# Keys multiplied once with a running maximum, and a ninth count table, in a graph, attention and expert layer on one core

## The chip, the cores and the metric

One core of a Trainium2 chip runs the whole layer in one launch. The metric is the device time of an execution in microseconds (us), the median of several; lower is better. The engines are PE (matrix products), DVE (vector), ACT (scalar functions), POOL (GpSimd) and SP, which here only issues transfers. Each has an instruction stream of its own, and streams wait for each other by semaphores.

## The reference, cut to what matters

```python
xn = layernorm(x)                                     # 6250 nodes x 256
# graph convolution: 100000 edges sorted by dst, plus one loop per node
out = segment_sum((xn @ W)[src] * norm[:, None], dst) + bias
gnn = prelu((out - out.mean()) / (out.std() + eps) * w + b)
# linear attention, 4 heads of 32, four memory keys and values ahead of the nodes'
q, k, v = split(rmsnorm(xn) @ w_qkv, 3)
q = softmax(q, over the 32 features) * 32 ** -0.5
k = softmax(k, over memory and all nodes)
context = sum over nodes of k * v                     # 32 x 32 a head
mix = rmsnorm(context applied to q, @ w_out + b_out) + xn
x = x + gnn + mix
x = x + top-2-of-8 experts(layernorm(x))
```

The edges are sorted by destination, and the low node numbers receive far more of them than the high ones.

## The kernel before, in words

The nodes are 49 tiles of 128 rows, the edges 196 groups of four chunks of 128. A first stage (to 125 us) counts degrees, normalises the rows, writes them to `table` in HBM and keeps them turned as `zT`. The second stage, the one that the change edits, sums neighbours' rows into `acc` and runs the attention beside that. A third applies `W` to `acc`, norms and routes; a fourth runs the experts (from about 920 us).

The second stage treats edge groups in two ways.

- **Tables** (groups 0 to 74, the dense ones). They are cut into eight blocks (`DBLK`). A block's destinations span at most 128 nodes, so its edges become a table of counts `adj`, 128 x 49 tiles x 128, which multiplies the rows of all nodes once. For each chunk of edges DVE makes two one-hot matrices in 16 bits (`chunk_onehots`, L1073 and L1074), PE multiplies them (`count`, L839), and DVE adds the narrow result into the table at a column that it reads from a register (`chunk_add`, L1088). When a block is complete, PE multiplies 49 tiles of the table by 49 tiles of `table` (`product`, L851), which SP loads again for each block into a ring `zrow` of six buffers (`z_rows`, L775). ACT copies the sum out (`block_out`, L1002), PE turns it (`turn_block`, L858), DVE adds it to `acc` (`add_block`, L1066). Two tables alternate; ACT wipes the part that was used (L958), and both whole tables at the start.
- **Steps** (the other 121 groups, `GQ`). For each, POOL gathers four times 128 rows of 1 KB by an indirect transfer (L811; the first two groups, `EARLY`, already at the end of the first stage, L466), into a ring of four groups. DVE makes a 128 x 4 x 96 one-hot (L1045), PE multiplies it with the gathered rows in two halves (`aggregate`, L828), DVE adds the 96-wide result to `acc` (`add`, L1058). POOL's gather for step q waits until PE has done step q - 4.

All other work is dealt out to the steps by hand: `share(q, lo, hi, n)` says which of n items fall to step q, `quarter` which to each quarter of it. The order on each engine is this list. `BUILT` says in which steps a block's chunks are counted, `USED` in which its products are made.

The attention, in the steps:

- From `A0` to `A1` (0 to 11) PE multiplies the keys of all tiles (L865) and DVE takes the maximum (L1099, at the first tile L1095). Two set-up steps turn the maximum into a row and multiply the memory's exponents.
- From `C0` to `C1` (14 to 33) PE multiplies keys and values again (L874), DVE subtracts the maximum (L1106), ACT takes the exponent (L974) and copies the values (L970), PE sums the context (L881).
- From `B0` to `B1` (37 to 87) the queries: two products and a transpose on PE (L888, L896, L902), six instructions on DVE, three on ACT.
- From `D0` to `D1` (91 to 118) the attention's norm; SP loads the tiles of x again into a ring of three (`x_tile`, L781, on the same queue as `z_rows`), ACT scales them (L994), DVE adds (L1154).

The last block is turned ahead of step 119, so its table rows, the last x tile and ACT's copy come ahead of the last aggregations on PE. After the loop SP loads the weights of the next stage; the third stage needs them and `acc`.

```python
BUILT = (0, 33, 47, 61, 74, 86, 95, 104, 112)
USED = (33, 47, 61, 74, 86, 95, 104, 112, GQ - 2)
```

## Time and profile before

| | |
|---|---|
| median of three runs | 1326.18 us (1324.99 to 1328.23) |
| the profiled execution's own time | 1320.53 us |
| its span | 1318.8 us |
| PE, DVE, ACT, POOL busy | 92%, 69%, 41%, 60% |
| second stage | from about 126 to 757 us |
| packets' bytes | 190.10 MB, mean 144 GB/s |

How to read it: the span goes from the first to the last instruction, and what lies around it makes up the execution's time. Busy shares count the time in which an engine executes; waiting and register instructions are left out. A float32 multiplication appears as two matmul records, and their durations overlap, so that what a record takes of PE is read from how closely they follow each other. In the chain of work a piece is followed back to what released it. "issue" is time in which an engine waited for nothing that the profile shows.

### The profile page before, as it was taken

The numbers are of one execution on the slowest core, as the hardware profiler recorded it, in microseconds if no ns is written. First come the engines' busy times: TensorE is split into PE (matmuls) and PEld (weight loads), VectorE is DVE, ScalarE is ACT, GpSimd is POOL, SyncE is SP. The second block draws the span as 40 slices with busy tenths as digits, with TensorE's granted clock in tenths as the row PEclk, the third lists the DMA queues.
The fourth block names the chain that finished last, engine by engine and source line by source line (L and its number), as shares of the span: only waits on it lengthen the run. The fifth ranks groups of instructions, "written<-read, shape, count | busy, mean of one in ns | idle before, by whom it ended". The sixth has DMA issues, their size and how long they took to land.

```text
span 1318.8 us, 29769 instructions
## 1 busy us (share of the span) xinstructions
PE 1206.9 (92%) x8357; PEld 1076.2 (82%) x8358; DVE 911.9 (69%) x2764; ACT 543.8 (41%) x1403; POOL 789.1 (60%) x757
## 2 busy tenths in 40 slices
PE   6974989998999999998998798958999999999998
PEld 6964978887889888887786646945999999999997
DVE  8997987887888778778784268888444444444444
ACT  8837102222333333333321102645555555555553
POOL 7105777777777777777777300003577666667665
PEclk9997999999999999999999899965999999999999
DMA  8026333336666667779998701578354444444443
GB/s 256 0 78 199 100 104 105 103 104 198 193 194 205 195 197 210 207 239 276 281 295 271 259 0 33 176 238 249 57 77 65 70 71 71 70 69 70 69 68 43
DMA packets 138889, 190.10 MB, mean 144 GB/s; under 512 B 22262, under 2 KB 116957, under 8 KB 138533
## 3 DMA queue, kind: packets, MB, share of 16 engines
q0 software_dynamic: 43440, 90.29, 29.6%
q1 hardware_dynamic: 95348, 98.64, 23.6%
q8 instruction: 43, 0.70, 0.2%
q14 instruction: 58, 0.47, 0.1%
HBM read 156.37 MB, written 33.44 MB: 144 GB/s over the span
## 4 chain that ended last, share of the span: by engine, by line
PE 54%; POOL 14%; DVE 9%; issue 7%; DMA 4%; DVEq 2%; ACT 1%; SPq 0%; POOLq 0%
PE ps L1991 14%; PE ps L2001 14%; POOL RG L811 14%; PE ps L828 7%; PE ps L851 4%; PE ps L1534 3%; DMA zrow<-table 2%; PE ps L1571 2%; PE ps L1981 2%; DVE R L1088 2%; PE ps L874 1%; PE ps L1589 1%; DMA RG<-table,srci 1%; PE ps L839 1%; DVEq L1080 1%
## 5 line engine op out<-in xcount | busy, mean ns | idle before, releaser
L811 POOL DMA_INDIRECT RG<-table,srci x476 | 468.4, 984 | 146.8 <-issue 142.9
L828 PEld LDWEIGHTS ps<-S_t,RG 128*128 128x128 f32 x1936 | 255.7, 196 | 21.5 <-DMA RG<-table,srci 11.4
L828 PE MATMUL ps<-S_t,RG 128*128 128x96 f32 x1936 | 258.9, 277 | 8.7 <-DMA RG<-table,srci 8.3
L851 PE MATMUL ps<-zrow,R 128*128 128x256 f32 (+1 forms) x784 | 220.8, 387 | 19.3 <-DMA zrow<-table 12.9
L2116 POOL DMA_INDIRECT out<-R,S_t x105 | 166.1, 1582 | 96.9 <-DVE R L2086 50.3
L1991 PE MATMUL ps<-R,RG 128*128 128x128 f32 x1680 | 204.9, 275 | 0.0
L2001 PE MATMUL ps<-R 128*128 x840 | 198.6, 380 | 0.0
L1991 PEld LDWEIGHTS ps<-R,RG 128*128 128x128 f32 x1680 | 195.9, 192 | 0.2 <-issue 0.2
L2028 ACT ACTIVATE R<-ps,RG 128x128 f32<-128x128 f32 x420 | 119.7, 368 | 177.1 <-PE ps L1991 177.1
L1088 DVE TENSOR_TENSOR R<-R,ps 128x245 f32 (+4 forms) x300 | 141.8, 473 | 69.4 <-PE ps L839 42.6
L2082 DVE TENSOR_TENSOR R<-ps,R 128x256 f32<-128x256 f32 x105 | 44.6, 425 | 202.0 <-PE ps L2001 202.0
L851 PEld LDWEIGHTS ps<-zrow,R 128*128 128x128 f32 (+1 forms) x784 | 135.4, 190 | 46.3 <-DMA zrow<-table 25.6
L2001 PEld LDWEIGHTS ps<-R 128*128 128x128 f32 x840 | 151.8, 191 | 16.2
L958 ACT ACTIVATE R<-iwin 128x256 f32<-128x256 f32 (+2 forms) x152 | 71.3, 476 | 183.7 <-PE ps L851 171.9
L2104 POOL DMA_INDIRECT R<-ntable,S_t x105 | 104.0, 991 | 38.7 <-issue 30.2
L2037 ACT ACTIVATE RG<-R 128x1028 f32 x105 | 112.7, 1075 | 4.1 <-DVEq L1918 4.1
L1684 POOL COPY R<-R 128x8 f32<-128x8 f32 (+1 forms) x13 | 6.5, 517 | 143.5 <-DVEq L1854 124.8
L2071 DVE TENSOR_SCALAR R<-ps,gamma,beta 128x128 f32<-128x128 f32 x212 | 76.0, 399 | 0.0
L487 PE MATMUL ps<-R 128*128 128x49 bf16 x784 | 73.8, 270 | 0.0
L487 PEld LDWEIGHTS ps<-R 128*128 128x128 bf16 x784 | 70.8, 145 | 2.8 <-DVE R L562 2.7
L1045 DVE TENSOR_TENSOR S_t<-dstrel,iwin 128x384 f32<-128x384 f32 x121 | 66.8, 552 | 0.8
L1074 DVE TENSOR_SCALAR ohs<-iokey,slo 128x128 bf16<-128x128 f16 x225 | 61.9, 275 | 0.0
(374 smaller groups left out, 1822.7 us busy)
## 6 DMA issues: line engine op xcount, KB each, us to landing
zrow<-table SPq DMA_DIRECT2D x384, 128.0 KB
RG<-table,srci POOLq DMA_INDIRECT x484, 3.3
ntable<-R SPq DMA_DIRECT2D x12, 516.0 KB, 6.6
out<-R SPq DMA_DIRECT2D x12, 512.0 KB, 3.2
table<-R SPq DMA_DIRECT2D x9, 640.0 KB
R<-in_x SPq DMA_DIRECT2D x6, 896.0 KB, 10.0
R<-in_w SPq DMA_DIRECT2D x8, 514.0 KB, 5.7
slot<-in_x SPq DMA_DIRECT2D x32, 128.0 KB
```

The costliest lines, as they stand in the source:

```text
L487: last = nc.tensor.matmul(ps[7][:, 0:T], ohlo[k][:, :, c], ohhi[k][:, :, c], start=False, stop=False)
L811: nc.gpsimd.indirect_dma_start(out=grows[:, s, :], out_offset=None, in_=table, in_offset=bass.IndirectOffsetOnAxis(ap=srci[:, ND + q, c:c ...
L828: last = nc.tensor.matmul(window(q % 2)[:, h, :], grows[:, s, h * P:(h + 1) * P], S_t[:, q % 2, c, :], start=c == 0, stop=c == GC - 1)
L851: nc.tensor.matmul(psD[:, 0:D], adj[b % 2][0:n, j, :], zrow[0:n, i % ZR, :], start=j == 0, stop=j == T - 1).then_inc(z_used, 1)
L1088: nc.vector.tensor_tensor(win, win, psK[m % 2][:, 0:T * wide].rearrange("p (j w) -> p j w", w=wide), ALU.add).then_inc(cnt_ok, 1)
L1991: last = nc.tensor.matmul(psH[s % 2][:, h * P:(h + 1) * P], w1r[:, s, k * HID + h * P:k * HID + (h + 1) * P], ur[:, s % 2, k, :], start=k ...
L2001: last = nc.tensor.matmul(psY[s % 2][:, 0:D], hr[:, s % 2, h, :], w2_sb[:, bass.ds(e, 1), h, :].rearrange("p a f -> p (a f)"), start=h == ...
L2028: last = act.activation(hr[:, s % 2, h, :], psH[s % 2][:, h * P:(h + 1) * P], ACT.Gelu, bias=w1r[:, s, KC * HID + h:KC * HID + h + 1])
L2037: act.activation(w1r[:, s, :], w1_sb[:, bass.ds(e, 1), :].rearrange("p a f -> p (a f)"), ACT.Copy).then_inc(c_ok, 1)
L2071: nc.vector.tensor_scalar(ur[:, s % 2, k, :], psX[s % 2][:, k * P:(k + 1) * P], gamma[:, k:k + 1], beta[:, k:k + 1], ALU.mult, ALU.add)
L2104: nc.gpsimd.indirect_dma_start(out=xr[:, t % 4, :], out_offset=None, in_=ntable, in_offset=bass.IndirectOffsetOnAxis(ap=gat[:, t:t + 1], a ...
L2116: nc.gpsimd.indirect_dma_start(out=a_out, out_offset=bass.IndirectOffsetOnAxis(ap=sct[:, t:t + 1], axis=0), in_=yr[:, t % 4, :], in_offset ...
```

## The change

Nothing outside the second stage is edited, but for one more block mask in the first stage.

- The groups 75 to 78 become a ninth table, nine columns wide; 117 steps and 468 gathers are left. `BUILT` and `USED` are written anew. `EARLY` is 1: one group's gathers are issued ahead of the barrier between the stages.
- Keys are multiplied once, turned (features on partitions) and in 13 rounds of four tiles. A round k begins at quarter 8 + 9k of the steps: PE multiplies 512 keys (quarter 0) and the values of its four tiles (1 to 4); DVE scales the keys by the nodes' norms, reduces the maximum and updates the running one (2); ACT takes the exponent and the factor by which older sums fade (3); PE turns the exponents (4); ACT copies them and the values (5); PE multiplies the context (7); DVE fades and adds (8).
- The norms, needed along the free dimension, are turned, stored to HBM and loaded as rows by SP into the ring of the table rows; SP begins with `z_rows` only after the last round. Exponents and values use the other buffers of the ring and the slots of x.
- The memory's maximum, exponents and products come first, ahead of the two wipes on ACT.
- The last block is turned after the last step.

```diff
-DBLK = ((0, 27), (27, 38), (38, 46), (46, 53), (53, 59), (59, 65), (65, 70), (70, 75))
+DBLK = ((0, 27), (27, 38), (38, 46), (46, 53), (53, 59), (59, 65), (65, 70), (70, 75), (75, 79))
-DWB = (5, 5, 6, 7, 8, 8, 8, 9)
+DWB = (5, 5, 6, 7, 8, 8, 8, 9, 9)
...
-        EARLY = 2
+        EARLY = 1
...
-        A0, A1 = 0, 12
-        C0, C1 = 14, 34
-        B0, B1 = 37, 88
-        D0, D1 = 91, GQ - 2
-        BUILT = (0, 33, 47, 61, 74, 86, 95, 104, 112)
-        USED = (33, 47, 61, 74, 86, 95, 104, 112, GQ - 2)
+        K0, KD = 8, 9
+        C1 = 32
+        B0, B1 = 35, 87
+        D0, D1 = 90, GQ - 2
+        BUILT = (0, 31, 43, 54, 64, 74, 84, 93, 101, 108)
+        USED = (31, 43, 54, 64, 74, 84, 93, 101, 108, GQ - 2)
...
+        def key_turn(q, r):
+            at = 4 * q + r - K0
+            return [(k, at - KD * k) for k in range(NKS) if 0 <= at - KD * k <= KD]
...
# SP
+                sp.wait_ge(cr_ok, 1)
+                sp.dma_start(cflat.rearrange("(t p) -> t p", p=P), ks4[0:T, 0:P]).then_inc(cr_out, 16)
+                sp.wait_ge(cr_out, 16)
+                for k in range(NKS):
+                    if k >= 2:
+                        sp.wait_ge(k_ok, k - 1)
+                    lo, n = KS * k * P, key_nodes(k)
+                    sp.dma_start(cq_row[k % 2][:, 0:n],
+                                 cflat[lo:lo + n].unsqueeze(0).to_broadcast([P, n])).then_inc(cr_in[k % 2], 16)
+                sp.wait_ge(cx_ok, NKS + 1)
                 for q in range(-2, GQ - 2):
                     for b, j in products(q + 2):
                         z_rows(b, j)
...
# PE
+                def keys(k):
+                    if k >= 1:
+                        pe.wait_ge(et_ok, k)
+                    lo, n = KS * k * P, key_nodes(k)
+                    for half in range(KC):
+                        last = nc.tensor.matmul(psKT[:, 0:n], wqkv[:, half, P:2 * P], zT[:, half, lo:lo + n],
+                                                start=half == 0, stop=half == KC - 1)
+                    last.then_inc(k_ps, 1)
+                def turn_exp(k):
+                    pe.wait_ge(ex_ok, k + 1)
+                    pe.wait_ge(k_top, k + 1)
+                    for j, t in enumerate(key_tiles(k)):
...
+                def context(k):
+                    pe.wait_ge(et_ok, k + 1)
+                    pe.wait_ge(v_ok, key_tiles(k)[-1] + 1)
+                    pe.wait_ge(cx_ok, k + 1)
...
                 def attention(q, r):
+                    if q == 0 and r == 0:
+                        nc.tensor.transpose(psT[0:T, :], cq[:, :], ident[:, :])
+                        pe.wait_ge(mem_ok, 1)
+                        nc.tensor.transpose(psKT[0:MEM, 0:P], emk, ident[:, :])
+                        nc.tensor.transpose(psKT[0:MEM, P:2 * P], mvv[:, :], ident[:, :]).then_inc(pre_pe, 1)
+                    if q == 0 and r == 3:
+                        pe.wait_ge(pre_dve, 1)
+                        nc.tensor.matmul(psC[:, 0:P + 1], emT[:, :], mvT[:, :], start=True, stop=True).then_inc(cx_ps, 1)
+                    for k, at in key_turn(q, r):
+                        if at == 0:
+                            if k == 0:
+                                pe.wait_ge(cr_ok, 1)
+                            keys(k)
+                        if 1 <= at <= len(key_tiles(k)):
+                            values(KS * k + at - 1)
+                        if at == 4:
+                            turn_exp(k)
+                        if at == 7:
+                            context(k)
...
                 for q in range(GQ):
-                    if q in USED[1:]:
+                    if q in USED[1:-1]:
                         turn_block(USED.index(q) - 1)
...
+                turn_block(NDB - 1)
# ACT
+                act.wait_ge(m_ok, 1)
+                act.activation(emk, mk[:, :], ACT.Exp, bias=negM[0]).then_inc(mem_ok, 1)
+                act.wait_ge(pre_pe, 1)
+                act.activation(ks4[0:T, 0:P], psT[0:T, :], ACT.Copy).then_inc(cr_ok, 1)
                 for b in range(2):
                     wipe(b, 0, T).then_inc(clear, 1)
...
+                def keys_exp(k):
+                    act.wait_ge(m_ok, k + 2)
+                    n = key_nodes(k)
+                    act.activation(fade[k % 2], negM[k % 2], ACT.Exp, scale=-1.0, bias=negM[(k + 1) % 2])
+                    act.activation(ks4[:, 0:n], ks4[:, 0:n], ACT.Exp, bias=negM[(k + 1) % 2]).then_inc(ex_ok, 1)
...
# DVE
+                def keys_scaled(k):
+                    n = key_nodes(k)
+                    v.wait_ge(k_ps, k + 1)
+                    v.wait_ge(cr_in[k % 2], k // 2 * 16 + 16)
+                    if k >= 1:
+                        v.wait_ge(et_ps, k)
+                    nc.vector.tensor_tensor(ks4[:, 0:n], psKT[:, 0:n], cq_row[k % 2][:, 0:n], ALU.mult).then_inc(k_ok, 1)
+                    v.wait_ge(k_ok, k + 1)
+                    nc.vector.tensor_reduce(ktop, ks4[:, 0:n], AX.X, ALU.max).then_inc(k_top, 1)
+                    v.wait_ge(k_top, k + 1)
+                    nc.vector.scalar_tensor_tensor(negM[(k + 1) % 2], ktop, -1.0, negM[k % 2], ALU.mult,
+                                                   ALU.min).then_inc(m_ok, 1)
+                    v.wait_ge(m_ok, k + 2)
+                def context_added(k):
+                    v.wait_ge(cx_ps, k + 2)
+                    v.wait_ge(ex_ok, k + 1)
+                    v.wait_ge(cx_ok, k + 1)
+                    nc.vector.scalar_tensor_tensor(ctx_s, ctx_s, fade[k % 2], psC[:, 0:P + 1], ALU.mult,
+                                                   ALU.add).then_inc(cx_ok, 1)
...
                 add(GQ - 1, blocks)
+                add_block(NDB - 1, GQ)
```

## Rows read from the trace of the kernel before

**Rows 1.** Grouped lines: line engine op names xcount | busy us, mean ns | idle before

```profile
L811 POOL DMA_INDIRECT RG<-table,srci x476 | 468.4, 984 | 146.8 <-issue 142.9 <-PE ps L828 2.4 <-POOLq L86 1.4
L1088 DVE TENSOR_TENSOR R<-R,ps 128x245 f32 (+4 forms) x300 | 141.8, 473 | 69.4 <-PE ps L839 42.6 <-issue 18.5 <-ACT R L958 2.2
...
L874 PE MATMUL ps<-wqkv,R 128*128 128x256 f32 x196 | 51.1, 383 | 0.0
L1074 DVE TENSOR_SCALAR ohs<-iokey,slo 128x128 bf16<-128x128 f16 x225 | 61.9, 275 | 0.0
...
L1106 DVE SCALAR_TENSOR_TENSOR ksl<-ps,cq,slotb 128x128 f32<-128x128 f32 x49 | 16.9, 346 | 0.8 <-PE ps L874 0.7
```

**Rows 2.** Waits of the whole span: waiter <- waited for: us, times, longest

```profile
PEld ps L828 <- DMA RG<-table,srci: 11.4, 18, 1.4
...
POOL RG L811 <- PE ps L828: 2.4, 6, 0.9
```

**Rows 3.** Windows: from:to us, busy per engine (xcount), then PEclk, DMA share, GB/s

```profile
137.70:177.10 39.40, 37.99 (x319) 34.98 (x318) 37.38 (x141) 0.00 (x0) 29.96 (x32) 1.00 0.35 102
...
332.70:362.80 30.10, 28.45 (x199) 24.86 (x199) 26.81 (x103) 10.48 (x34) 22.78 (x25) 1.00 0.66 196
388.50:429.20 40.70, 40.61 (x291) 38.15 (x290) 33.91 (x131) 15.64 (x53) 31.07 (x32) 1.00 0.67 201
...
620.00:640.00 20.00, 19.29 (x122) 16.67 (x122) 16.90 (x52) 8.27 (x20) 15.43 (x16) 1.00 0.97 306
...
659.60:690.30 30.70, 30.07 (x184) 26.14 (x184) 27.13 (x78) 6.44 (x11) 23.38 (x25) 1.00 0.94 293
704.20:735.40 31.20, 27.56 (x151) 21.23 (x150) 10.82 (x28) 5.08 (x9) 23.89 (x25) 1.00 0.93 286
```

**Rows 4.** Windows of line 828 alone: PE and PEld busy (xrecords), PEclk, DMA share, GB/s

```profile
126.00:300.00 174.00, 71.20 (x536) 67.47 (x537) 0.96 0.37 108
...
332.70:362.80 30.10, 12.33 (x96) 12.63 (x97) 1.00 0.66 196
388.50:429.20 40.70, 18.69 (x144) 18.94 (x144) 1.00 0.67 201
659.60:690.30 30.70, 12.73 (x96) 12.77 (x97) 1.00 0.94 293
704.20:735.40 31.20, 10.28 (x80) 10.50 (x80) 1.00 0.93 286
```

**Rows 5.** Timeline, the stage's start and POOL's last gather: start us, us, instruction

```profile
123.77 0.94 POOL L466 DMA_INDIRECT RG<-table,srci  x1 [0.30 <-issue]
125.52 5.43 ACT L958 ACTIVATE R<-iwin 128x6272 f32<-128x6272 f32 x1 [7.70 <-PEq L86]
...
130.43 0.39 PE L839 MATMUL ps<-ohk,ohs 128*128 128x245 bf16 x1 [17.45 <-DVE ohs L1074]
131.16 0.42 DVE L1088 TENSOR_TENSOR R<-R,ps 128x245 f32 x1
...
738.94 0.95 POOL L811 DMA_INDIRECT RG<-table,srci  x1 [0.30 <-issue]
```

**Rows 6.** Chain that ended last, in the stage's last steps: start us, us, what

```profile
735.05 4.97 DMA zrow<-table
...
741.48 7.92 DMA slot<-in_x
...
751.04 6.10 PE ps L828 x32
```

**Rows 7.** The same chain in the expert stage, where PE runs full

```profile
925.67 1.73 PE ps L2001 x8
927.62 1.79 PE ps L1991 x16
```

**Rows 8.** Grouped lines of the later stages: 512-wide work on DVE and ACT

```profile
L1634 ACT ACTIVATE R<-R,small 128x512 f32<-128x512 f32 (+1 forms) x26 | 18.8, 777 | 2.0 <-DVEq L1762 2.0
...
L1705 DVE TENSOR_TENSOR R<-ps,R 128x500 f32<-128x500 f32 (+1 forms) x26 | 15.9, 652 | 13.4 <-PE ps L1534 13.4
```

More of the change, by code:

```diff
@@ L96, in build @@
         o_all = x_all
-        adj = [R1[:, b * T * P:(b + 1) * T * P].rearrange("p (j n) -> p j n", n=P) for b in range(2)]
+        adj = [R1[:, (b + NDB) % 2 * T * P:((b + NDB) % 2 + 1) * T * P].rearrange("p (j n) -> p j n", n=P) for b in range(2)]
         def o_tile(t):
@@ new lines, in values @@
+                def values(t):
+                    if t >= KS:
+                        pe.wait_ge(v_ok, t - KS + 1)
+                    j = t % KS
+                    for half in range(KC):
+                        last = nc.tensor.matmul(psV[:, j * P:(j + 1) * P], zT[:, half, t * P:(t + 1) * P],
+                                                wqkv[:, half, 2 * P:3 * P], start=half == 0, stop=half == KC - 1)
+                    last.then_inc(v_ps, 1)
+                def turn_exp(k):
+                    pe.wait_ge(ex_ok, k + 1)
+                    pe.wait_ge(k_top, k + 1)
+                    for j, t in enumerate(key_tiles(k)):
+                        n = P if t < T - 1 else TAIL
+                        last = nc.tensor.transpose(psKT[0:n, j * P:(j + 1) * P], ks4[:, j * P:j * P + n], ident[:, :])
+                    last.then_inc(et_ps, 1)
@@ new lines, in context @@
+                def context(k):
+                    pe.wait_ge(et_ok, k + 1)
+                    pe.wait_ge(v_ok, key_tiles(k)[-1] + 1)
+                    pe.wait_ge(cx_ok, k + 1)
+                    tiles = key_tiles(k)
+                    for j, t in enumerate(tiles):
+                        n = P if t < T - 1 else TAIL
+                        last = nc.tensor.matmul(psC[:, 0:P + 1], et4[0:n, j * P:(j + 1) * P], v4[0:n, j, :], start=j == 0,
+                                                stop=t == tiles[-1])
+                    last.then_inc(cx_ps, 1)
@@ L904, in attention @@
                 def attention(q, r):
-                    for t in quarter(share(q, A0, A1, T), r):
-                        keys(t)
-                    if q == A1 and r == 2:
-                        pe.wait_ge(mid_dve, 1)
-                        nc.tensor.transpose(psC[:, 0:P], cn, ident[:, :]).then_inc(mid_pe, 1)
-                    if q == A1 + 1 and r == 2:
-                        pe.wait_ge(mid_dve, 2)
-                        nc.tensor.matmul(psA[1][:, 0:P], ones[:, :], cn, start=True, stop=True).then_inc(mid_pe, 1)
-                        pe.wait_ge(mem_ok, 1)
-                        nc.tensor.transpose(psA[0][0:MEM, 0:P], emk, ident[:, :])
-                        nc.tensor.transpose(psA[0][0:MEM, P:2 * P], mvv[:, :], ident[:, :]).then_inc(mid_pe, 1)
@@ L916, in attention @@
-                    if q == C0 and r == 0:
-                        pe.wait_ge(mid_dve, 3)
-                        nc.tensor.matmul(psC[:, 0:P + 1], emT[:, :], mvT[:, :], start=True, stop=False,
-                                         skip_group_check=True)
-                    for s in quarter(share(q, C0, C1, T + 1), r):
-                        if s < T:
-                            keys_values(s)
-                        if s >= 1:
-                            context(s - 1)
-                    if q == C1 + 1 and r == 2:
-                        pe.wait_ge(mid_dve, 4)
+                    if q == 0 and r == 0:
[3 more added lines that the diff above has]
+                        nc.tensor.transpose(psKT[0:MEM, P:2 * P], mvv[:, :], ident[:, :]).then_inc(pre_pe, 1)
```

170 lines of the change are left out of this document (76 added, 94 removed).

## The prediction

> **What bounds the kernel now.** I read four views in this order. The page's busy shares average over stages with different limits, so they only say where to look: the change touches one stage alone, the gather steps, from about 126 to 757 us. There the grouped lines [rows 1] give the gathers: 476 of them, 468.4 us busy and 146.8 us idle before them, nearly all "issue". That is 1.29 us for each, 5.17 us for a step of four. The waits [rows 2] show who sets the pace: POOL waited for PE six times, 2.4 us in all, and PE waited for a gather only 18 times in 121 steps. So POOL never stops, and PE runs a little behind it, with a lag that the ring of four groups tolerates. The windows [rows 3], cut at starts of groups, and most of them again for the aggregation alone [rows 4] (16 records are one step) say how close PE is. From 388.5 to 429.2 it was busy 40.61 of 40.70 us and did nine steps, 4.52 us each with 3.5 table products and nearly one query tile: PE at its limit, catching up on POOL. From 332.7 to 362.8 it needed 5.02 us for equal products, because DVE (26.81 of 30.10 us busy, plus its register loads) had 3.1 count chunks per step. From 659.6 to 690.3 a step took 5.12 us with 6.1 products, from 704.2 to 735.4 it took 6.24 us with 7: there PE is idle again and waits for table rows. POOL issued its last gather at 738.94 [rows 5], yet the stage closed at 757, after a row load, an x tile and four groups [rows 6]. So POOL sets the pace in the middle, and PE or the row stream at the end.
>
> **The change part by part**, as shifts of the end of this stage; what lies behind it is not edited. A matmul record takes PE 0.216 us at 256 columns and 0.112 at 128 [rows 7]; a float32 multiplication is two records.
>
> *Sixteen gathers fewer* free POOL by 16 x 1.29 = 20.7 us. This is a gain only as far as POOL sets the pace, so it isn't booked as such; the sum below goes by PE and DVE.
>
> *The start.* One group instead of two ahead of the barrier: the others waited for POOL there (its last early gather began at 123.77, ACT and DVE went on at 125.5 [rows 5]), so they start four gathers, 5.0 us, earlier. But the two wipes of the tables now stand behind memory exponent, transposes and norms: DVE's set-up (4.9 us from the barrier to the first count at 130.43), three transposes and a copy (some 1.8 us), then the wipe of 5.43 us. The exponent itself and its table load lie beside DVE's five microseconds. The first table addition moves from 131.16 to about 120.5 + 4.9 + 1.8 + 5.5 = 132.7. Behind it come two copies and one product that PE waits for, 1 us: **+2.5 us** (0 to +4).
>
> *The key stage.* Removed: 196 key-and-value records of 256 columns and as many key records of 128, 42 and 22 us of PE slots, 49 DVE instructions of 0.346 us [rows 1] and 48 of the same form for the maximum, 33.5 us. Added on PE, per round of four tiles: four records of 512 columns at 0.43 (twice the 256 form), 16 of 128, four transposes, eight context records, 4.9 us, 13 rounds less the short tail, 61 us: PE gains nothing worth naming. Added on DVE per round: a 512-wide product with PSUM (0.65 [rows 8]), a reduction of the same width (taken as 0.65 too; the trace has none of that shape, the product bounds it from above, half of it from below), a column operation and the fading sum (0.35 as a key instruction), with the hand-overs 1.9 us, 24 us in all. DVE saves 9 us, a third of which I take as path because PE is nearly as full: **-3 us** (-9 to +20, rival two). Until 300 us PE did 33.5 steps [rows 4], 4.9 us each after the first; products now begin at step 31 instead of 33: **-9.8 us** of lead. ACT takes an exponent of 512 (0.78 [rows 8]) and two kinds of copies, beside a PE that has longer work; they are hidden unless a round is late. On SP a norm store and 13 broadcast loads come first; nothing else is due on that queue. But the row ring holds norms until the last round, so table rows, which were prefetched, are asked for only at step 31: PE stands for one load, **+3.5 us** (0 to 5; a row load on the chain took 4.97 [rows 6]).
>
> *The ninth table.* 49 products more at 0.43: +21.2 us of PE. Two steps fewer with products (86 for 88) at 1.75 a group: -3.5. Sixteen counts more, between 0.1 and 0.37 us: +3. Their DVE chunks go beside PE. Of this **+20.7**, PE can take what it stood behind POOL: from step 61 to 104 it needed on average 4.6 us (4.52 at 3.5 products, 0.43 for each beyond, and, once the queries are through, 0.98 less: five of 128 columns and two of 256 for a tile) where POOL gave 5.17: 43 x 0.56 = **-24 us**. What it loses again: steps 35 to 43 have 3.67 chunks each where DVE was full at 3.1; half a chunk (an addition of 0.47 and two one-hots of 0.28 or more, overlapping [rows 1]; 0.9 taken), eight steps, **+4**; one more change of block, and fuller steps at the others, **+2**. In steps 54 to 84 PE now needs 4.52 + 1.4 x 0.43 and wider counts, 5.2 to 5.3 us: no slack is left there. Bounds: all slack used and no loss gives -3, none used +21. 25 more wipes lie on ACT, whose wipes follow PE's products, beside them; 49 more row loads lie on SP.
>
> *The last steps.* Two blocks instead of one are used at seven rows a step. By the windows the blocks of 8, 7 and 7 steps take 41 + 44 + 44 us where PE needs 39 + 36 + 34, 20 us less; before, those of 8 and 7 took 41 + 44 where it needed 39 + 33, 13 less. So the stream costs some 6 us more; gathers held back by PE leave it some room: **+3** (-8 to +8).
>
> *The last turn* goes behind all groups. The four groups that stood behind it took 6.10 us [rows 6]; but the next stage also waits for weights that SP asks for two groups from the end, and these came 9 us later, as now: **-0.6** (-4 to 0).
>
> Sum: 2.5 - 3 - 9.8 + 3.5 + 20.7 - 24 + 4 + 2 + 3 - 0.6 = -1.7 us. It is worked out against the profiled execution, 1320.53 us (span 1318.8); the median shown, 1326.18, is 0.4% above it, and I take the same shift from the median: **1324.5 us**.
>
> **The rivals.** *One: POOL stays the pace to the end.* Then 20.7 less the 2.5 of the start come off: -18 us, 1308. For it: POOL hardly ever waited, and the middle had 24 us of slack. Against it: PE was saturated for nine steps already, and the last 14 steps ask for 7 rows, 2 x tiles and 4 gathers, 13 x 128 KB in 5.17 us, 329 GB/s, where the fullest window shows 306 at a DMA share of 0.97 [rows 3]. It decides if a step of seven rows takes under 5.5 us. The Trainium skill ("DMA: Bandwidth & Descriptors", Specifications) puts the limit of HBM for one core at about 358 GB/s; by that the last steps would keep POOL's pace and this rival would come true, while the windows, 286 to 306 GB/s at shares of 0.93 to 0.97, speak against it.
>
> *Two: the key rounds hold PE and DVE up.* A round passes PE, DVE (three instructions that wait on each other), ACT and PE again within four quarters of a step. PE runs up to two chunks ahead of DVE, so it can arrive at the transposes while DVE and ACT still have 1.9 + 1 us to do; what DVE then cannot fill with counted chunks is lost to both. At 1.5 us a round, 13 rounds cost 19.5 us, and the steps behind have no slack for it: +18, **slower, 1344**. It decides above 0.45 us a round. For it: the three dependent DVE steps, and DVE, busy 37.38 of 39.40 us while the keys were read the first time [rows 3]. Against it: four quarters are 5 us, and PE's work per step falls short of POOL's.
>
> *Three: the change doesn't do what it says.* If an edge falls outside the ninth table's nine columns, the repair pass over all groups runs, hundreds of us. The same test held for the eighth table at nine columns; one in a hundred.
>
> **How the numbers follow.** Forecast 0.47, rival one 0.28, rival two 0.24, rival three 0.01. A change of 0.3% (4 us) is about what a measurement can tell. The forecast's own range, by its bounds, is 1315 to 1334; half of it lies within 4 us, a quarter on either side. Faster: 0.28 + 0.11 = 0.39; same 0.25; slower 0.24 + 0.11 + 0.01 = 0.36. Two in ten may lie outside; the range reaches nearly to both rivals: 1307 to 1341.
>
> **What would show it.** First table addition near 132.7 us; products some 4 us earlier than now; POOL waiting for PE in the middle, 15 us or more in all instead of 2.4 (rival one: again a few us); steps 54 to 84 at 5.3 us with PE full; the steps of seven rows at 6.0 to 6.3 us; PE waits at the transposes of the rounds under 0.45 us each (rival two: over 1). Wrong would be a stage end more than 8 us from 756, and the sum with it.

## The result, and the profile after

The changed kernel takes 1351.77 us (median of 4 runs, 1350.3 to 1353.94) against 1325.59 us of the kernel before (4 runs on the same chip): a ratio of 1.0197, 95% interval 1.0176 to 1.0217. It is slower by 26 us; the forecast was 1324.5, the range 1307 to 1341. Its profiled execution spans 1348.7 us, 29.9 more than that of the kernel before, which lay 5 us under its own median (1320.53 us), where the changed kernel's lay 1.4 us under.

The head of its page and the chain of work (before: PE 92%, POOL 60% busy, and a chain with 54% PE and 14% POOL):

```profile
span 1348.7 us, 29739 instructions
...
PE 1209.3 (90%) x8312; PEld 1067.1 (79%) x8313; DVE 926.2 (69%) x2756; ACT 556.8 (41%) x1420; POOL 771.8 (57%) x742
...
PE 64%; DVE 12%; DMA 8%; issue 3%; DVEq 2%; ACT 1%; SPq 0%; POOL 0%; POOLq 0%
```

POOL has left the chain; PE, DVE and DMA have taken its place, yet PE's busy time is nearly the same (1209 and 1207 us). Of the 29.9 us, 27.5 are time in which PE stands. The grouped lines that answer to [rows 1] and the waits that answer to [rows 2] say behind whom:

```profile
L849 POOL DMA_INDIRECT RG<-table,srci x464 | 450.7, 971 | 195.4 <-issue 118.9 <-PE ps L866 75.1 <-POOLq L89 1.4
...
L889 PE MATMUL ps<-zrow,R 128*128 128x256 f32 x882 | 247.2, 390 | 29.9 <-DMA zrow<-table 22.4 <-DVE R L1132 5.9 <-DVEq L1258 1.2
...
L1154 DVE TENSOR_TENSOR R<-R,ps 128x245 f32 (+4 forms) x316 | 151.8, 480 | 84.0 <-PE ps L877 48.3 <-issue 14.9 <-ACT R L1010 8.4
```

```profile
POOL RG L849 <- PE ps L866: 75.1, 74, 4.8
...
DVE R L1154 <- PE ps L877: 48.3, 73, 3.9
...
PE ps L889 <- DMA zrow<-table: 22.4, 26, 4.0
...
PE ps L877 <- DVE R L1154: 19.3, 27, 4.5
...
PE ps L922 <- ACT kesl L1022: 16.6, 13, 1.9
...
PE ps L1595 <- DMA RG<-in_lnb: 6.4, 1, 6.4
```

POOL waited for PE 75.1 us instead of 2.4: the gathers that were saved are off the path. PE itself waits for table rows, for table additions, at the transposes of the key rounds (13 times, 1.3 us each), and once before the next stage.

Where in the stage the time went is read from the ends of the steps (the start of the 16th aggregation record of each step in the timeline, from the same zero as [rows 3]; steps are counted from 0). "First product" is the first one with table rows, in step 33 before and in step 31 after:

| stretch | before, us | after, us | difference |
|---|---|---|---|
| first group aggregated, at | 136.4 | 137.8 | +1.4 |
| from there to the first product | 159.0 | 164.3 | +5.3 |
| first product to the last group | 461.5 | 477.3 | +15.8 |
| last group to the next stage's first record | 1.8 | 6.9 | +5.1 |
| first 16 records of the next stage | 6.97 | 8.98 | +2.0 |

These make 29.6 of the 29.9 us. The last two groups are in the third line, and they took 4.2 us where the kernel before needed 8.3. So the fourth line tells little alone: from the start of the last two groups to the next stage it is 10.2 us before and 11.1 after, 0.9 more, and from the first product to the start of the last two groups 20.0 more.

Windows of the changed kernel cut at ends of steps (steps 1 to 30; 31 to 33; 54 to 83; 84 to 100; 101 to 114), in the columns of [rows 3]:

```profile
137.80:297.50 159.70, 134.91 (x982) 115.48 (x982) 126.94 (x424) 31.73 (x89) 113.47 (x119) 0.97 0.41 114
297.50:317.60 20.10, 14.08 (x85) 11.91 (x85) 11.91 (x47) 2.50 (x6) 12.74 (x14) 0.80 0.65 193
426.40:588.80 162.40, 159.13 (x1069) 145.82 (x1069) 136.50 (x475) 58.11 (x198) 115.07 (x121) 1.00 0.74 219
588.80:680.70 91.90, 84.51 (x523) 73.37 (x522) 71.08 (x207) 33.39 (x84) 68.35 (x68) 1.00 0.87 266
680.70:775.30 94.60, 80.89 (x443) 65.57 (x442) 49.97 (x133) 17.23 (x32) 52.05 (x52) 0.96 0.84 256
```

In the first stretch, with keys and counts alone, PE stands 24.8 of 159.7 us. The same 30 steps of the kernel before took 147.5, with 7.6 us of standing:

```profile
136.40:283.90 147.50, 139.92 (x1018) 125.36 (x1017) 124.92 (x451) 25.12 (x86) 112.26 (x115) 0.99 0.36 103
```

Steps 54 to 83 show PE at its limit (159.13 of 162.40 us), 5.41 us a step; in the last steps it stands again, 13.7 of 94.6 us, while the core's DMA engines are 0.87 and 0.84 busy in the last two of these windows. The engines aren't full there: SP, which asks for the rows, waited 40.7 of the 94.6 us until PE had used a buffer of the row ring.

One key round as VectorE's timeline shows it, from the last addition ahead of the round to the first behind it:

```profile
244.12 0.41 DVE L1154 TENSOR_TENSOR R<-R,ps 128x245 f32 x1 [0.47 <-PE ps L877]
244.45 0.28 DVE L1139 TENSOR_SCALAR slot<-iokey,dstrel 128x245 bf16<-128x245 f16 x1
244.64 0.43 DVE L1140 TENSOR_SCALAR ohs<-iokey,slo 128x128 bf16<-128x128 f16 x1
244.80 0.68 DVE L1163 TENSOR_TENSOR kesl<-ps,zrow 128x512 f32<-128x512 f32 x1
245.52 0.69 DVE L1165 TENSOR_REDUCE small<-kesl 128x1 f32<-128x512 f32 x1
246.24 0.16 DVE L1167 SCALAR_TENSOR_TENSOR small<-small 128x1 f32<-128x1 f32 x1
246.44 0.56 DVE L1111 TENSOR_TENSOR S_t<-dstrel,iwin 128x384 f32<-128x384 f32 x1
247.62 0.41 DVE L1154 TENSOR_TENSOR R<-R,ps 128x245 f32 x1 [0.62 <-issue]
```

Between additions that otherwise follow each other in 0.91 us lie 3.5 us. PE's timeline of the same moment has the gap at the transposes:

```profile
245.48 0.61 PE L913 MATMUL ps<-wqkv,R 128*128 128x128 f32 x4
247.40 0.65 PE L922 MATMUL ps<-ident,kesl 128*128 128x128 f32 x4 [1.30 <-ACT kesl L1022]
248.17 0.27 PE L877 MATMUL ps<-slot,ohs 128*128 128x245 bf16 x1
...
302.15 1.22 PE L889 MATMUL ps<-zrow,R 128*128 128x256 f32 x2 [4.04 <-DMA zrow<-table]
...
779.55 0.38 PE L896 MATMUL ps<-ident,R 128*128 128x128 f32 x2
786.33 8.98 PE L1595 MATMUL ps<-R,RG 128*128 128x500 f32 x16 [6.39 <-DMA RG<-in_lnb]
```

The last three lines are the wait for the first table rows and the one before the next stage.

### The profile page after: what moved, and what is told of

Its sections match the earlier page's. It is cut to its first block, busy times and chain, and to the rows that moved or that the text cites. A ratio compares the mean times of both kernels' runs of the same rounds, so it can differ in the third digit from the quotient of the medians.

```text
span 1348.7 us, 29739 instructions
## 1 busy us (share of the span) xinstructions
PE 1209.3 (90%) x8312; PEld 1067.1 (79%) x8313; DVE 926.2 (69%) x2756; ACT 556.8 (41%) x1420; POOL 771.8 (57%) x742
## 4 chain that ended last, share of the span: by engine, by line
PE 64%; DVE 12%; DMA 8%; issue 3%; DVEq 2%; ACT 1%; SPq 0%; POOL 0%; POOLq 0%
PE ps L2052 14%; PE ps L2062 13%; PE ps L889 10%; PE ps L866 9%; DMA zrow<-table 6%; PE ps L1595 3%; DVE R L1154 3%; PE ps L877 2%; PE ps L1632 2%; PE ps L2042 2%; PE ps L954 1%; PE ps L940 1%; PE ps L1650 1%; DMA slot<-in_x 1%; DVEq L1146 1%
## 5 line engine op out<-in xcount | busy, mean ns | idle before, releaser
L849 POOL DMA_INDIRECT RG<-table,srci x464 | 450.7, 971 | 195.4 <-issue 118.9
L889 PE MATMUL ps<-zrow,R 128*128 128x256 f32 x882 | 247.2, 390 | 29.9 <-DMA zrow<-table 22.4
L866 PEld LDWEIGHTS ps<-S_t,RG 128*128 128x128 f32 x1872 | 248.0, 197 | 13.0 <-issue 3.1
L866 PE MATMUL ps<-S_t,RG 128*128 128x96 f32 x1872 | 247.7, 277 | 0.3 <-DVE S_t L1111 0.3
L1154 DVE TENSOR_TENSOR R<-R,ps 128x245 f32 (+4 forms) x316 | 151.8, 480 | 84.0 <-PE ps L877 48.3
L889 PEld LDWEIGHTS ps<-zrow,R 128*128 128x128 f32 x882 | 154.5, 192 | 63.9 <-DMA zrow<-table 37.1
L1010 ACT ACTIVATE R<-iwin 128x256 f32<-128x256 f32 (+2 forms) x177 | 81.8, 467 | 217.2 <-PE ps L889 212.6
L877 PE MATMUL ps<-ohk,ohs 128*128 128x245 bf16 (+4 forms) x158 | 47.7, 304 | 21.4 <-DVE ohs L1140 12.9
L1140 DVE TENSOR_SCALAR ohs<-iokey,slo 128x128 bf16<-128x128 f16 x237 | 66.0, 278 | 0.0
```

The lines of the kernel that those rows point to most:

```text
L849: nc.gpsimd.indirect_dma_start(out=grows[:, s, :], out_offset=None, in_=table, in_offset=bass.IndirectOffsetOnAxis(ap=srci[:, ND + q, c:c ...
L866: last = nc.tensor.matmul(window(q % 2)[:, h, :], grows[:, s, h * P:(h + 1) * P], S_t[:, q % 2, c, :], start=c == 0, stop=c == GC - 1)
L889: nc.tensor.matmul(psD[:, 0:D], adj[b % 2][0:n, j, :], zrow[0:n, i % ZR, :], start=j == 0, stop=j == T - 1).then_inc(z_used, 1)
L1010: return act.activation(adj[b % 2][:, j:j + n, :], iwin[:, :].unsqueeze(1).to_broadcast([P, n, P]), ACT.Copy, scale=0.0)
L1154: nc.vector.tensor_tensor(win, win, psK[m % 2][:, 0:T * wide].rearrange("p (j w) -> p j w", w=wide), ALU.add).then_inc(cnt_ok, 1)
```

## The experiments

Times are medians; ratios are to runs of the kernel before on the same chip. Theories: *one*, hand-overs in the key rounds; *two*, first that the ninth table is the loss, then, once that was split up, that VectorE is held in the rounds; *three*, the row stream.

**The two halves alone.** The changed kernel with the tables of before, then the kernel before with the tables of the changed one:

```diff
-DBLK = (..., (65, 70), (70, 75), (75, 79))
+DBLK = (..., (65, 70), (70, 75))
 ...
-BUILT = (0, 31, 43, 54, 64, 74, 84, 93, 101, 108)
+BUILT = (0, 33, 47, 61, 74, 86, 95, 104, 112)
```

> The one-pass keys alone, with the eight tables, the 121 steps and the due steps of the kernel before. Theory one (hand-overs: in each key round TensorE stands 1.3 us at the transposes for ScalarE's exponent, 16.6 us over 13 rounds, and GpSimd's ring is held back with it): GpSimd, which set the pace before and has no slack to catch up with 121 steps, ends as late as it was held, so 1332 to 1340 us. Theory two (the keys cost nothing that lasts, the ninth table's products are what made the kernel slower): 1322 to 1328 us.

Measured 1337.52 us, ratio 1.0089 (1.0063 to 1.0115), in the range of theory one. Only the 11 us are shown by it, not the mechanism. Its six executions spread from 1328.9 to 1342.3 us, and the trace is of the fastest.

```diff
-DBLK = (..., (65, 70), (70, 75))
+DBLK = (..., (65, 70), (70, 75), (75, 79))
 ...
-USED = (33, 47, 61, 74, 86, 95, 104, 112, GQ - 2)
+USED = (31, 43, 54, 64, 74, 84, 93, 101, 108, GQ - 2)
```

> The ninth table alone, with keys multiplied twice as before. Theory one (the key rounds are the loss, the table is about even: 20.7 us of TensorE more against 20.7 us of GpSimd less): 1320 to 1330 us. Theory two (the table is the loss: TensorE and the row loads become the bound from step 31 on): 1336 to 1350 us.

Measured 1347.08 us, ratio 1.0161 (1.0137 to 1.0185). This is the range of theory two. Each half is a loss, some 11 and 20.5 us; together they would be 31.5, and are 26. Both lengthen the key stage (first 30 steps 156.9 and 155.4 us, both 159.7, before 147.5), which is where they overlap. The table costs more than the keys. It also took away its own lead: with the keys as before, 31 steps take 163.1 us here, where the kernel before took 164.4 for 33. The first table's 108 chunks are the same in number; two steps fewer only make the steps denser. A chunk takes 1.49 us of the first 30 steps here and 1.50 in the kernel before.

**The wait at the transposes.** They are moved two quarter-steps on, the context product and the fading sum behind them one, and the rounds begin two earlier:

```diff
-        K0, KD = 8, 9
+        K0, KD = 6, 9
 ...
-                        if at == 4:
+                        if at == 6:
                             turn_exp(k)
-                        if at == 7:
+                        if at == 8:
                             context(k)
 ...
```

> The changed kernel with the transposes of the exponents two quarter-steps later behind ScalarE's exponent (and all that follows in the round, with the rounds begun two quarter-steps earlier). Theory one (hand-overs): TensorE's wait at the transposes falls from 16.6 us to under 4, the first step with products ends 9 to 13 us earlier than 307.6, and the time falls to 1337 to 1343 us. Rival (VectorE's load in the key rounds is the limit): the wait moves to the counts and the table additions, the first step with products ends no more than 4 us earlier, and the time stays at 1347 to 1352 us.

Measured 1364.38 us, ratio 1.0272 (1.0241 to 1.0304): slower still. From 126 to 300 us no wait at the transposes is left; PE waits for additions instead, where the changed kernel had 11.6 us of that in 126 to 298:

```profile
PE ps L877 <- DVE R L1155: 29.1, 26, 4.5
...
DVE R L1155 <- PE ps L877: 24.9, 26, 2.8
```

So theory one falls: with the transposes out of the way PE stands no less, and what it waits for is VectorE. That the time even rises shows in the window of the first 30 steps:

```profile
141.10:313.00 171.90, 142.69 (x981) 122.72 (x981) 125.61 (x421) 31.78 (x89) 113.53 (x119) 0.92 0.38 107
```

981 records take 142.69 us at a granted clock of 0.92, against 134.91 for 982 at 0.97 in the changed kernel: 7.8 of the 12.2 us more are PE's own records running longer. The other 4.4 us are standing: 29.2 us instead of 24.8.

**VectorE's block, and VectorE's work.** First, in the kernel with the late transposes, the round's three instructions stand apart:

```diff
 ...
                         if at == 2:
                             keys_scaled(k)
+                        if at == 3:
+                            keys_largest(k)
+                        if at == 4:
+                            keys_max(k)
```

> As the run with the late transposes (1364.4 us), but VectorE's product, reduction and running maximum of a key round stand in three successive quarter-steps, with count additions between them, and the exponent one quarter-step later. Theory two (VectorE is held for 2.45 us in one piece in each round, while TensorE may run only two counts ahead): TensorE's waits for additions fall from 29.1 to under 12 us, the first 30 steps take under 158 us (171.9 there, 159.7 in the changed kernel), and the time is 1340 to 1350 us. Rival (the sum of VectorE's work, or TensorE's clock once it has stood, sets the pace of the key stage): the first 30 steps take over 165 us and the time stays at 1356 to 1366 us.

Measured 1350.37 us, ratio 1.0177 (1.0134 to 1.022); the first 30 steps take 159.4 us. Their window, and waits from 126 to 300 us:

```profile
141.00:300.40 159.40, 139.12 (x982) 120.57 (x981) 120.79 (x420) 30.70 (x89) 111.35 (x117) 0.93 0.40 113
...
PE ps L922 <- ACT kesl L1022: 14.6, 13, 1.8
...
PE ps L877 <- DVE R L1155: 10.2, 10, 4.5
```

The waits for additions fall as theory two has it, but the one at the transposes is back, and the 159.4 us are those of the changed kernel (159.7); the median lies just above theory two's range. PE stands 20.3 us, 8.9 less than with the late transposes and the block in one piece and 4.5 less than in the changed kernel; against the latter its records run 4.2 us longer, at a granted clock of 0.93. So some of the standing comes from VectorE's block being in one piece, most of it stays when the block is split, and in the time nothing is gained over the changed kernel. The trace is of the slowest of the five executions (1359.01 us). Then, in the changed kernel itself, the reduction is left out:

```diff
-                    nc.vector.tensor_reduce(ktop, ks4[:, 0:n], AX.X, ALU.max).then_inc(k_top, 1)
+                    v.sem_inc(k_top, 1)
```

> The changed kernel without VectorE's reduction of a key round (0.72 us and a hand-over of 0.17 of the 1.8 us that product, reduction and running maximum hold VectorE); the maximum stays that of the memory keys, so the numbers that come out are others. If it is VectorE's held time that paces the key stage: the first 30 steps fall from 159.7 by 8 to 11 us (12 rounds of 0.89), and since TensorE is full behind them the time falls to 1340 to 1345 us. Rival (the rounds wait on something else: ScalarE, the ring, the clock): no more than 4 us less in these steps, 1347 to 1353 us.

Measured 1342.67 us, ratio 1.0142 (1.0105 to 1.0179), 9.1 below the changed kernel. Its window of the first 30 steps, and waits from 126 to 300 us:

```profile
141.10:289.90 148.80, 131.32 (x982) 111.92 (x981) 116.64 (x408) 31.74 (x89) 112.27 (x118) 0.99 0.42 122
...
PE ps L877 <- DVE R L1154: 12.0, 15, 4.5
...
PE ps L922 <- ACT kesl L1022: 9.2, 12, 1.3
```

148.8 us, 10.9 less, though not one instruction of PE, ACT or POOL is gone. That this is VectorE's held time (12 x 0.89 = 10.7) to the tenth is partly luck: 7.3 us of it are standing (17.5 us instead of 24.8), and 3.6 are PE's records running faster as the clock rises from 0.97 to 0.99. The standing is the firmer figure. In the seven executions with the changed kernel's first 30 steps the time swings from 159.3 to 164.3 us with the clock (0.97 to 0.94), but PE stands 24.2 to 25.1 us in each; in both without the reduction it stands 17.2 and 17.5. So VectorE's time in a round holds PE up. By which way it does is not settled by this run: the waits for additions stay (11.6 and 12.0 us), and what falls is the wait at the transposes (16.6 to 9.2), since the reduction is also a link of the chain that they wait for. Both together, late transposes and no reduction, were not run.

**The row stream.**

```diff
-                    sp.dma_start(zrow[0:n, i % ZR, :], table[j * P:j * P + n, :])
+                    w = D if i < ZR else D // 4
+                    sp.dma_start(zrow[0:n, i % ZR, 0:w], table[j * P:j * P + n, 0:w])
```

> The changed kernel with only the first 64 of 256 columns of each table-row tile loaded (after the first six tiles); the products are as many and as wide, so the output is not the reference's. Theory three (the row stream, 128 KB a product, sets the pace where seven or eight products fall on a step): steps 100 to 114 fall from 6.6 to 5.3 to 5.6 us, TensorE's 22 us of waits for rows fall under 6, and the time falls to 1328 to 1338 us. Rival (TensorE's own work sets that pace): no more than 4 us less, 1347 to 1352 us.

Measured 1333.18 us, ratio 1.0051 (1.0035 to 1.0068): 18.6 less. The windows of this kernel, 134 us of the middle and steps 93 to 114:

```profile
432.00:566.00 134.00, 131.83 (x887) 120.87 (x886) 113.26 (x397) 48.45 (x166) 95.84 (x101) 1.00 0.48 129
...
636.30:756.40 120.10, 113.97 (x690) 99.91 (x689) 86.62 (x239) 35.13 (x72) 90.26 (x89) 1.00 0.69 188
```

and those of the changed kernel:

```profile
426.00:560.00 134.00, 131.84 (x887) 120.82 (x886) 113.25 (x396) 48.55 (x166) 95.74 (x101) 1.00 0.73 217
...
635.50:775.30 139.80, 121.99 (x691) 100.62 (x689) 88.37 (x242) 35.18 (x74) 85.67 (x85) 0.98 0.87 266
```

In the middle nothing changes, to 0.01 us of PE's time: PE is the bound and rows are hidden. In the last 22 steps 139.8 us become 120.1, and in the nine before them, with 5.4 rows a step, 46.7 become 43.0. The gain lies there, 23.4 us; the stretches ahead and behind took some us more in this execution. What narrow rows change is both the bytes and how soon a row lands; a longer ring was not run, so which of the two holds the steps up is open. An edit that keeps the result is fewer rows a step at the end:

```diff
...
-        USED = (31, 43, 54, 64, 74, 84, 93, 101, 108, GQ - 2)
+        USED = (31, 42, 52, 62, 72, 81, 90, 99, 107, GQ - 2)
```

> The changed kernel with the products of the last tables spread over more steps: the tables' last steps are 31, 42, 52, 62, 72, 81, 90, 99, 107 and 115, so that no step has over 6.1 products (7 and 8 before). Theory three (the row stream is full at seven rows a step): 1337 to 1345 us. Rival (TensorE is full in the steps that now get more products, so that these lose what the last ones gain): 1347 to 1353 us.

Measured 1344.13 us, ratio 1.0113 (1.0067 to 1.0159). Steps 93 to 114 take 122.7 us, 17.1 less, but steps 34 to 92, where PE is full, 5.0 more. The execution also came 3.2 us later to its first step and took 2.3 more for the first 30, whose code is the changed kernel's.

**The waits at either end of the products.**

```diff
+                sp.wait_ge(k_ok, NKS)
-                sp.wait_ge(cx_ok, NKS + 1)
 ...
+                    if i == 4:
+                        sp.wait_ge(cx_ok, NKS + 1)
```

> The changed kernel with the first four table-row tiles asked for as soon as the last keys are scaled, some 1.5 steps ahead of the first product, instead of behind the last context. If TensorE's stop at step 31 is a row load that comes too late (a gap of some 5 us, predicted 3.5): step 31 takes 5 to 7 us instead of 10.1, and the time is 1345 to 1349 us. Rival (the gap is absorbed further on): 1350 to 1353 us.

Measured 1349.27 us, ratio 1.017 (1.0128 to 1.0213). Step 31 takes 5.4 us instead of 10.1, so the gap was the late rows; of the 4.7 us some 2.5 reach the end, by medians that overlap: a small gain, not settled in size.

```diff
-                sp.wait_ge(pe_done, GQ - 2)
+                sp.wait_ge(pe_done, GQ - 3)
```

> The changed kernel with the next stage's weights asked for one step earlier (their place in the ring of gathered rows is free by then). If the last table's turn was shortened for nothing because the next stage waits 6.4 us for its weights: that wait goes and the time is 1344 to 1347 us. Rival (the weights then share the DMA engines with the last row tiles, which come later by as much): 1349 to 1353 us.

Measured 1352.31 us, ratio 1.0182 (1.0129 to 1.0236): nothing. The wait before the next stage is again 6.39 us. The DMA issues of its last microseconds (KB, us from issue to landing) show why:

```profile
R<-dflat SPq DMA_DIRECT2D x1, 3125.0 KB, 15.5
...
RG<-in_gw SPq DMA_DIRECT2D x1, 256.0 KB, 11.3
...
RG<-in_lnb SPq DMA_DIRECT2D x1, 1.0 KB, 13.5
```

The weights are asked for right behind a broadcast of one row of norms to all partitions, 3.1 MB, and share the engines with it. Asked for earlier, they land no earlier. What PE waits for is the last of the four loads, `in_lnb`, 1 KB: it took 9.2 us in the changed kernel, 7.6 in the kernel before. Now they go ahead of the broadcast:

```diff
-                sp.wait_ge(blk_t, NDB - 1)
-                sp.dma_start(dall, dflat[0:N].unsqueeze(0).to_broadcast([P, N])).then_inc(da_in, 16)
-                sp.wait_ge(pe_done, GQ - 2)
+                sp.wait_ge(pe_done, GQ - 3)
                 sp.dma_start(gw, ...).then_inc(gw_in, 16)
 ...
+                sp.wait_ge(blk_t, NDB - 1)
+                sp.dma_start(dall, dflat[0:N].unsqueeze(0).to_broadcast([P, N])).then_inc(da_in, 16)
```

> The changed kernel with the next stage's weights asked for ahead of the broadcast of the norms (3.1 MB, 15 us from issue to landing) and not behind it. If the 6.4 us that TensorE stands before the next stage are this broadcast's share of the DMA engines: the gap falls under 2.5 us and the time is 1345 to 1348 us. Rival (the next stage then waits for the broadcast instead): 1350 to 1356 us.

Measured 1344.36 us, ratio 1.014 (1.0106 to 1.0174). The profiled execution was the longest of its four (1354.4), but the gap is read from it all the same: its issues, and PE's first record of the next stage in the timeline:

```profile
R<-dflat SPq DMA_DIRECT2D x1, 3125.0 KB, 12.4
RG<-in_gw SPq DMA_DIRECT2D x1, 256.0 KB, 3.0
...
RG<-in_lnb SPq DMA_DIRECT2D x1, 1.0 KB, 5.8
```

```profile
788.91 8.67 PE L1595 MATMUL ps<-R,RG 128*128 128x500 f32 x16 [2.19 <-DVEq L1421]
```

The weights take 3.0 us to landing in place of 6.2 in the changed kernel, `in_lnb` 5.8 in place of 9.2, and the gap is 2.2 us in place of 6.4. The 7.4 us by which the median fell are more than this gap explains: in this execution the last two groups ran longer (7.3 us instead of 4.2), and from their start to the next stage it took 10.1 us against 11.1. The mended kernel below, with the same edit, took 6.7.

**Do the parts add up?** First no reduction and narrow rows at once:

> The changed kernel with both edits at once: no reduction in the key rounds (alone 9.1 us less, at 1342.7) and narrow row loads (alone 18.6 us less, at 1333.2); the output is not the reference's. If VectorE's held time in the key stage and the row stream in the later steps are two separate losses, in different stretches: their sum, 1324.1, so 1320 to 1328 us. Rival (they overlap, because GpSimd's or TensorE's pace is met once one of them is gone): 1330 to 1336 us.

Measured 1322.55 us, ratio 0.9959 (0.9942 to 0.9976): the sum, 1324.1, within the noise. The two losses are separate. With both edits PE's waits for rows are 7.6 us and POOL's for PE still 38.8.

Then the three edits that keep the result:

> The changed kernel with the three complete edits that helped: products spread (alone 1344.1), first row tiles asked for earlier (1349.3), weights ahead of the broadcast (1344.4). If the losses at the first product, in the last steps and behind the last one are separate: 1351.8 - 7.6 - 2.5 - 7.4 = 1334.3, so 1331 to 1338 us. Rival (less row traffic in the last steps already lets weights and broadcast land in time): 1339 to 1344 us.

Measured 1335.26 us, ratio 1.0057 (1.0037 to 1.0077): again the sum. The changed kernel, mended in three places, stays behind the kernel before.

**The same in the kernel before.** Narrow rows, then its products spread:

> The kernel before with only the first 64 of 256 columns of each table-row tile loaded (after the first six), so the output is not the reference's. Theory three: the steps 92 to 118 fall to 134 to 138 us and the time to 1308 to 1316 us, less than the 18.6 us that the same edit gave in the changed kernel, since GpSimd's pace is a floor here. Rival (rows bound the changed kernel alone): 1322 to 1328 us.

Measured 1322.93 us, ratio 0.9976 (0.9957 to 0.9994): 3 us where the changed kernel gave 18.6. Steps 93 to 118 take 143.7 us instead of 150.8, not the 134 that POOL would allow, and the last two groups 13.8 instead of 8.3. So rows bound mainly the changed kernel.

```diff
...
-        USED = (33, 47, 61, 74, 86, 95, 104, 112, GQ - 2)
+        USED = (33, 47, 59, 70, 80, 90, 100, 110, GQ - 2)
```

> The kernel before, with the products of its eight tables spread more evenly: the tables' last steps 33, 47, 59, 70, 80, 90, 100, 110 and 119 in place of 33, 47, 61, 74, 86, 95, 104, 112 and 119, so that the last two tables take 4.9 and 5.4 products a step and not 6.1 and 7. Theory three (the row stream is the bound of the last steps in that kernel too, and GpSimd the bound of the middle): the 26 steps from 92 to 118 fall from 150.8 towards GpSimd's 134 us, 1311 to 1319 us. Rival (the middle, which now has more products, gives up as much): 1323 to 1329 us.

Measured 1321.19 us (12 runs), ratio 0.9975 (0.9957 to 0.9992): between the two expectations. Steps 93 to 118 take 132.8 us, now at POOL's pace; but the steps from 34 to 92 take 5.5 more, and the last two groups 15.3 instead of 8.3, because at the end PE stands for the copy of the last table's sum (4.2 us; 1.4 in the kernel before) and for gathers, as its timeline says:

```profile
737.77 0.46 PE L828 MATMUL ps<-S_t,RG 128*128 128x96 f32 x2 [1.73 <-DMA RG<-table,srci]
...
744.73 0.69 PE L858 MATMUL ps<-ident,R 128*128 128x128 f32 x2 [4.21 <-ACT R L1002]
...
748.91 3.34 PE L828 MATMUL ps<-S_t,RG 128*128 128x96 f32 x14 [2.53 <-DMA RG<-table,srci]
752.65 3.30 PE L828 MATMUL ps<-S_t,RG 128*128 128x96 f32 x14 [0.39 <-DMA RG<-table,srci]
```

Last, the weights ahead of the broadcast as well:

> The kernel before with products spread (alone 1321.2) and the weights ahead of the broadcast. In the spread kernel TensorE waits at the end for gathers (2.5 us and 0.4 us) and for the copy of the last table's sum (4.2 us), not for rows or weights. If GpSimd's gathers close the stage: no more than 3 us less, 1318 to 1323 us. Rival (the broadcast slows the last gathers and the last rows): 1311 to 1317 us.

Measured 1322.12 us, ratio 0.9955 (0.9938 to 0.9973): the weights add nothing, and the last two groups again take 15.3 us. That POOL closes the stage fits this and the range, but no run shows it alone. These two are the fastest kernels of the study that compute the whole, 0.25% and 0.45% below the kernel before; their intervals overlap.

## Why the prediction was wrong, point by point

*The start* was right: +1.4 us for +2.5, the first table addition at 132.91 for 132.7. The agreement is closer than the runs allow: among executions with the same code up to there, the end of the first step swings by some 4 us (136.4 to 140.6 for the kernel before's, 137.4 to 141.2 for the changed one's).

*The key stage and the lead* failed first. By the sum's terms (2.5 - 3 - 9.8 + 3.5) the first product was to come 6.8 us earlier; it came at 302.1 instead of 295.4, 6.7 later. Two steps of the working are at fault. The lead took 4.9 us a step over from the kernel before, as if the pace belonged to the step. By the run with the table alone it goes with the first table's chunks, of which each step now holds 3.5 instead of 3.3: with the old keys, that run kept 1.3 of the 9.8 us. And the key term booked a gain of 3 us because VectorE's work in sum falls by 9; the run with the new keys alone shows the first 30 steps 9.4 us longer (156.9 for 147.5). The term took a round's work on VectorE to lie beside PE, and it holds PE up: PE stood 21.9 us there instead of 7.6, and leaving the reduction out of the changed kernel took 7.3 us of standing and 10.9 us in all away for 10.7 left out. The reduction, taken as 0.65 us, took 0.686: the size was right, its place was not. The Trainium skill ("VectorE: DVE Perf Modes", the section on the TRN2 errata) gives 691 ns for a float32 sum of two tensors at 512 elements; the trace agrees for the product of two tensors of that width, 0.681 us.

*Rival two* (1344) named the place, the hand-overs of a round, and its mark was met: 1.3 us at the transposes, where it decided above 0.45. The transposes alone are not the cause: with that wait taken away there it came back at the counts, and the time rose. Its price for the key stage, +18, is not far from the 13.5 us by which the first product missed the forecast. Its mechanism, VectorE's and ScalarE's time in a round lost to PE, is borne out as far as VectorE's part goes.

*The table rows* at step 31: +3.5 booked, 4.04 and 4.7 us measured. Right.

*The ninth table* in the middle was right: steps 54 to 83 at 5.41 us with PE full, 5.2 to 5.3 plus changes of block booked. POOL's slack was used up as booked, and POOL waited 75 us.

*The last steps* failed second. Booked were 6.0 to 6.3 us a step with seven rows and +3 in all; steps 101 to 114 took 6.76, and narrow rows gave back 19.7 us over steps 93 to 114. For these 22 steps the working had 41 + 44 + 44 = 129 us, and they took 139.8. From the first product on, 5.7 us were booked for table and last steps together, 15.8 came, and 20.0 without the last two groups. The step that failed took the pace of single windows of the kernel before, five and six steps long, for a stretch of 22 in which PE was already late. *Rival one* (1308) fell with this: seven rows a step were to take under 5.5 us. The window of steps 93 to 114 moved 266 GB/s at a share of 0.87, and the same steps of the mended kernel, with its products spread, 290 at 0.93:

```profile
645.80:764.50 118.70, 108.58 (x651) 91.67 (x649) 79.99 (x219) 30.80 (x64) 88.85 (x86) 1.00 0.93 290
```

By the 358 GB/s that the Trainium skill gives for one core ("DMA: Bandwidth & Descriptors", Specifications) these steps would have kept POOL's pace. The trace does not agree for rows and gathers: neither these windows nor the fullest of [rows 3], 306 GB/s at 0.97, reach it, and the measurement decides. (Five us with the broadcast under way, 775 to 780 of the changed kernel, show 367.)

*The last turn* was to gain 0.6 us "as the weights come later, as now". They came later than that: from the moment they are asked for to the landing of the last it is 10.7 us, 9.1 before. The gap before the next stage grew by 5.1 us, but the last two groups ahead of it took 4.2 less, so the turn itself missed by 1.5 us: +0.9 for -0.6. The term looked at when the weights are asked for, not at the 3.1 MB ahead of them in the same queue, which are what delays them.

In the next stage the first records take 2.0 us longer, at a mean granted clock of 0.77 instead of 1.00; no term had that. It is not the gap's doing alone: the kernel before with its products spread has the old gap of 1.58 us, and there these records take 8.6 us at 0.81.

Sum of the misses: 13.5 to the first product, 14.3 from there to the last two groups, 1.5 from there to the next stage, 2.0 in it, 31.3 of the 31.6 us between -1.7 booked and 29.9 measured. The runs without the reduction and with narrow rows show the two largest causes, and taken away in one kernel these come off in full; the runs with rows asked for ahead and with the weights first show two small ones.

Open: why the late transposes cost more than the changed kernel (7.8 of 12.2 us are the clock, but what made it fall is not shown); whether a round holds PE up through VectorE's queue or through the chain of hand-overs; whether bytes or the ring of six buffers hold up the last steps; and what paces the key stage with the old keys and the denser counts, where PE stands 11.8 of 155.4 us.

## What to carry to other kernels

A step is not a unit of time: before booking a gain for fewer steps, ask which engine's work per step grows, and take the pace from that work. Where two engines lean on each other through a pair of buffers, the wait shows where the order of the program puts it; leave some work out of the suspected engine before moving the wait about. A stream that kept up in a short window of the old kernel isn't free in a longer one of the new; price it over the stretch and at the density that it will have. Compare stretches by how long the engine stands, apart from how long its records run: the standing in the first 30 steps came out the same to 1 us in seven executions, while the time moved by 5 with the clock.

## What was not expected of the hardware

A broadcast of one 25 KB row to 128 partitions (3.1 MB) took 12.4 to 15.5 us to land and slowed what was asked for behind it: 256 KB of weights took 3.0 and 3.8 us ahead of it, 4.5 to 11.3 behind, and a 1 KB load 5.8 and 6.5 ahead, 7.6 to 13.5 behind. TensorE's granted clock fell to 0.92 over 172 us of the kernel with late transposes, although none of PE's waits in it from 141 to 313 us was longer than 2.2 us; its 30 waits for additions there make 29.0 us.
